# Attention inputs of all four sequences in one stage, and the last mixture, norm and store of all four sequences in one stage

## The chip, the cores and the metric

The kernel runs on one core of a Trainium2 chip. The metric is the device time of one launch in microseconds (us). Before the change it is 2777.98 us, the median of three runs (2776.31 to 2781.35).

## What is computed

The input x holds 4 sequences of 1024 positions with 128 features. It passes through four residual blocks, each of which works on the layer-normalised x: a gated linear recurrence with a feed-forward part, a mixture of 16 experts of which each position uses two, a softmax attention with rotary positions, and a last block with its own attention, a norm and a mixture of 8 experts. Cut to what matters here:

```python
x = x + _L0_attn_ref(_layernorm(x), ...)          # recurrence and feed-forward
x = x + _L0_ffn_ref(_layernorm(x), ...)           # 16 experts, two per position
x = x + _L1_attn_ref(_layernorm(x), ...)          # attention, 16 heads of 8
x = x + _L1_ffn_ref(_layernorm(x), ...)           # attention, norm, 8 experts, norm
...
q, k = _rope(proj(Wq, bq)), _rope(proj(Wk, bk))
v = proj(Wv, bv)
scores = jnp.einsum('bhtd,bhsd->bhts', q, k) / scale
out = jnp.einsum('bhts,bhsd->bhtd', jax.nn.softmax(scores, axis=-1), v)
...
x1 = _layernorm(x + attn_out, g1, be1)
return _layernorm(x1 + moe_out, g2, be2)
```

## The kernel before

The program is a row of **stages**. A stage (`stage`, L65) opens semaphores, gives each engine a block of instructions, and ends with a barrier of all engines (L78), after which GpSimd's (POOL's) `sem_clear` has freed the semaphores. Inside a stage each engine goes through its own instructions strictly in the order written, and waits only on semaphores. Engines are PE (TensorE), DVE (VectorE), ACT (ScalarE), POOL (GpSimd) and SP (the queue that issues the direct DMAs).

Both layers of attention run through L1235 to L1284. "Layer 0" below is the first of the two, "layer 1" the second. A layer has these stages before attention proper:

1. The first (L1252): SP loads `cos` and `sin`, in layer 0 DVE sets two rows that SP stores eight times, and POOL fills `v_ext` with ones (L1274).
2. In layer 0 alone, `fetch_first` (L1220): POOL gathers the experts' answers of sequence 0, 16 indirect DMAs (`fetch`, L611), and waits for them.
3. `attention_inputs(b)` (L709), once per sequence. DVE first combines the gathered answers with x in layer 0 (`combine`, L621: 8 + 8 instructions on `w_now`), then computes the norm (`norm_vector`, L96). PE transposes the 8 tiles of `xn` (`norm_tensor`), ACT copies them to `y_t` in two halves, PE projects four **jobs** (q and k, each in two halves of 512 positions; two matmuls of 512 columns per job, L736), then v (L739). DVE turns each job by the rotary angles (`ra` L756, `rb` L759, `rot` L764). ACT rounds `rot` to the high part (`qh`, `kh`, L810), POOL subtracts it for the low part (`ql`, `kl`, L784), and SP stores the parts to the DRAM tensor `qk_parts`, six DMAs of 512 KB per sequence. The buffers `ra`, `rb`, `rot` hold two jobs, so that DVE starts job n only after POOL has made the low part of job n - 2:

```python
                if n >= 2:
                    dve.wait_ge(summed, n - 1)
                    dve.wait_ge(low, n - 1)
```

POOL's order in this stage is: the 16 gathers of the next sequence (layer 0), or in the last sequence the memsets of `qs` and `ks` (L790, L791), then the residual plus bias (L794), then the four low parts, and at last a wait for the gathers.

Attention proper (L850) is one stage for all sequences, and starts with SP's loads from `qk_parts` (L881, L882). Its end and the second mixture of experts follow. The end of the program is `fetch_first` again, and then `finish(b)` (L677), one stage per sequence: DVE combines, norms, scales and adds (L705), SP stores, while POOL gathers the answers of the next sequence and waits for them.

Of the kernel before, what the change touches and what calls it, by code (L numbers as in the profile page):

```python
# [14 lines left out]
P = 128  # L15
# [13 lines left out]
PART_STORES = 6  # L29
# [139 lines left out]
def take_low_inputs(dve, t, high):  # L169

    for h in range(NH):
        dve.wait_ge(high, h + 1)
        s = slice(h * HALF, (h + 1) * HALF)
        dve.tensor_tensor(t["y_low"][:, s], t["y_f"][:, s], t["y_high"][:, s].bitcast(F32), ALU.subtract)

# [435 lines left out]
def fetch(pool, t, b):  # L611

    for i in range(NT):
        for k in range(2):
            pool.indirect_dma_start(t["back"][:, b % 2, i, k, :], None, t["answers"],  # L615
                                    bass.IndirectOffsetOnAxis(ap=t["slot_of"][:, b * NT + i, k:k + 1], axis=0))\
                .then_inc(t["fetched"], 16)
            t["fetches"] += 16

def combine(dve, t, b, copied, mixed, out, base):  # L621

    dve.tensor_copy(t["w_now"][:, :, :], t["wt"][:, bass.ds(b * NT, NT), :]).then_inc(copied, 1)  # L623
    dve.wait_ge(copied, 1)
    for i in range(NT):
        dve.scalar_tensor_tensor(t["mixed"][:, i, :], t["back"][:, b % 2, i, 0, :], t["w_now"][:, i, 0:1],  # L626
                                 base(i, 1).rearrange("p a d -> p (a d)"), ALU.mult, ALU.add).then_inc(mixed, 1)
    for i in range(NT):
        dve.wait_ge(mixed, i + 1)
        dve.scalar_tensor_tensor(out(i, 1).rearrange("p a d -> p (a d)"), t["back"][:, b % 2, i, 1, :],  # L630
                                 t["w_now"][:, i, 1:2], t["mixed"][:, i, :], ALU.mult, ALU.add).then_inc(mixed, 1)
    dve.wait_ge(mixed, 2 * NT)
# [44 lines left out]
def finish(nc, t, b):  # L677

    xn, x2, x = t["xn"], t["x2"], t["x"]  # L680
    with stage(nc, *NORM, "copied", "mixed", "added") as (block, *sems, copied, mixed, added):
        @block.sync
        def _(sp):
            for h in range(NH):
                sp.wait_ge(added, h + 1)
                sp.dma_start(t["out_v"][b, :, h * TPH:(h + 1) * TPH, :], x(h * TPH, TPH))\
                    .then_inc(t["out_stored"], 16)

        @block.gpsimd
        def _(pool):  # L690
            if b + 1 < B:
                fetch(pool, t, b + 1)
                pool.wait_ge(t["fetched"], t["fetches"])

        @block.scalar
        def _(act):
            norm_scalar_root(act, t, sems)

        @block.vector
        def _(dve):  # L700
            combine(dve, t, b, copied, mixed, lambda i, n: xn[:, i:i + n, :], t["n_view"])
            norm_vector(dve, t, sems, xn, x2, row_gain=t["row"]("g2"), row_shift=t["row"]("be2"))
            dve.wait_ge(sems[3], NT)
            for h in range(NH):
                dve.tensor_tensor(x(h * TPH, TPH), x(h * TPH, TPH), x2[:, h * TPH:(h + 1) * TPH, :],  # L705
                                  ALU.add).then_inc(added, 1)

def attention_inputs(nc, t, w, layer, a, b):  # L709
# [4 lines left out]
    jobs = [(k, h) for k in range(2) for h in range(NH)]  # L714
    with stage(nc, *NORM, "proj_done", "rot_used", "summed", "high", "low", "v_done", "rot_a", "copied", "mixed") as \
            (block, *sems, proj_done, rot_used, summed, high, low, v_done, rot_a, copied, mixed):

        stored, before = t["parts_stored"], PART_STORES * 16 * (B * layer + b)

        @block.sync  # L720
        def _(sp):
            for k, (first, second, third) in enumerate((("qh", "qh", "ql"), ("kh", "kl", "kh"))):
                for i, part in enumerate((first, second, third)):
                    sp.wait_ge(low if part in ("ql", "kl") else high, NH * (k + 1))
                    sp.dma_start(t["parts"][b, k, :, i * DH:(i + 1) * DH, :],
                                 a[part][:, :].bitcast(F32)).then_inc(stored, 16)

        @block.tensor
        def _(pe):
            norm_tensor(pe, t, sems, t["xn"], 6)  # L730
            for n, (k, h) in enumerate(jobs):
                if n >= 2:
                    pe.wait_ge(rot_used, n - 1)
                pe.wait_ge(sems[5], h + 1)
                for i, m in enumerate(((wq, wqr), (wk, wkr))[k]):
                    pe.matmul(psum[:, 2 * (n % 2) + i, :], m, t["y_t"][:, h * HALF:(h + 1) * HALF],  # L736
                              start=True, stop=True).then_inc(proj_done, 1)
            for i in range(NT):
                last = pe.matmul(psum[:, 4 + i // TPH, (i % TPH) * P:(i % TPH + 1) * P], t["y_t"][:, i * P:(i + 1) * P],  # L739
                                 wv, start=True, stop=True)  # L740
                if i % TPH == TPH - 1:
                    last.then_inc(v_done, 1)

        @block.vector
        def _(dve):
            if layer == 0:
                combine(dve, t, b, copied, mixed, t["x"], t["x"])
            norm_vector(dve, t, sems, t["x"](), t["xn"])
            for n, (k, h) in enumerate(jobs):
                s = slice(h * HALF, (h + 1) * HALF)  # L750
                name = "qk"[k]
                dve.wait_ge(proj_done, 2 * n + 1)
                if n >= 2:
                    dve.wait_ge(summed, n - 1)
                    dve.wait_ge(low, n - 1)
                dve.scalar_tensor_tensor(a["ra"][:, n % 2, :], psum[:, 2 * (n % 2), :], col(f"att{layer}_b{name}"),  # L756
                                         t["cos"][:, s], ALU.add, ALU.mult).then_inc(rot_a, 1)
                dve.wait_ge(proj_done, 2 * n + 2)
                dve.scalar_tensor_tensor(a["rb"][:, n % 2, :], psum[:, 2 * (n % 2) + 1, :],  # L759
                                         col(f"att{layer}_b{name}r"), t["sin"][:, s],  # L760
                                         ALU.add, ALU.mult).then_inc(rot_used, 1)
                dve.wait_ge(rot_a, n + 1)
                dve.wait_ge(rot_used, n + 1)
                dve.tensor_tensor(a["rot"][:, n % 2, :], a["ra"][:, n % 2, :], a["rb"][:, n % 2, :],  # L764
                                  ALU.add).then_inc(summed, 1)
            for h in range(NH):
                dve.wait_ge(v_done, h + 1)
                bias = t["rows"][:, ROWS[f"att{layer}_bv"]:ROWS[f"att{layer}_bv"] + 1, :].to_broadcast([P, TPH, D])
                dve.tensor_tensor(t["v_ext"][:, b * NT + h * TPH:b * NT + (h + 1) * TPH, 0:HEADS * VE]
                                  .rearrange("p i (h c) -> p i h c", c=VE)[:, :, :, 0:DH],  # L770
                                  psum[:, 4 + h, :].rearrange("p (i h d) -> p i h d", i=TPH, d=DH),
# [610 lines left out]
```

## Time and profile before

| what | value |
|---|---|
| median of three runs | 2777.98 us |
| the profiled execution's own time | 2800.65 us |
| its span, first to last instruction | 2799.4 us |
| PE, DVE, ACT, POOL busy share | 78%, 75%, 54%, 18% |
| DVE maxima in attention (L1048) | 1253.9 us in 2048 instructions |
| ACT exponentials in attention (L1028) | 1110.8 us in 2048 instructions |
| POOL gathers of answers (L615) | 133.2 us in 128 instructions |
| POOL memsets of `v_ext`, `qs`, `ks` (L1274, L790, L791), mean of one | 4551, 3511, 6950 ns, two of each |
| projections (L736), mean of one record | 702 ns, 128 records |

In the timeline a row such as "x8" merges equal instructions that follow each other; a wait of DVE on PEq or POOLq at L69 or L78 is the barrier between two stages.

### The profile page before, as it was taken

To read this page: it belongs to the slowest core of one execution; us is meant where nothing else is said; L and a number is where in the kernel's file an instruction comes from. 1 tells how busy PE (TensorE), PEld (TensorE's weight loads), DVE (VectorE), ACT (ScalarE), POOL (GpSimd) and SP (SyncE) were. 2 spreads that over 40 slices of the span, in tenths; PEclk is the share of its full clock that TensorE was granted. 3 is DMA by queue.
4 is the path that set the end of the run, shared out by engine and by line. 5 is a ranking of instruction groups with operands and counts; after the bars stand their busy time and mean duration, and the time that the engine had idled before them with its cause. 6 is when DMAs were issued, how large, how long until landed. Compare 5 with 4: busy or idle time off the path is not lost. (4 is left out here: it accounts for less than half of the span.)

```text
span 2799.4 us, 47294 instructions
## 1 busy us (share of the span) xinstructions
PE 2189.5 (78%) x17224; PEld 1196.2 (43%) x17224; DVE 2107.7 (75%) x4605; ACT 1502.4 (54%) x2898; POOL 504.2 (18%) x410
## 2 busy tenths in 40 slices
PE   6888965772339999999999549999999999458910
PEld 5667744661123333333333223333333333348910
DVE  6667767462568999999996568999999997375635
ACT  4433430240105888888888215888888888304510
POOL 2223310555630000000000230000000000006544
PEclk9999975896657999999999767999999999658965
DMA  4000000242330000000000330000000000202211
GB/s 173 0 0 0 0 24 14 68 82 73 117 112 13 25 14 25 25 14 25 20 7 1 106 121 17 25 13 25 22 17 25 13 14 2 97 8 62 68 45 53
DMA packets 64576, 109.71 MB, mean 39 GB/s; under 512 B 10352, under 2 KB 44272, under 8 KB 64112
## 3 DMA queue, kind: packets, MB, share of 16 engines
q1 hardware_dynamic: 55408, 88.60, 9.3%
q0 software_dynamic: 8960, 18.37, 2.7%
q8 instruction: 127, 2.08, 0.3%
q14 instruction: 81, 0.66, 0.1%
HBM read 64.46 MB, written 41.94 MB: 38 GB/s over the span
## 5 line engine op out<-in xcount | busy, mean ns | idle before, releaser
L1048 DVE TENSOR_REDUCE mh<-psum 128x1 f32<-128x512 f32 x2048 | 1253.9, 682 | 87.2 <-PE psum L923 78.1
L1028 ACT ACTIVATE p<-psum 128x512 f32<-128x512 f32 x2048 | 1110.8, 596 | 205.9 <-PE psum L957 168.1
L923 PE MATMUL psum<-ks,qs 64*128 64x512 f32 x2048 | 767.2, 462 | 35.0 <-DMA ks<-qk_parts 34.3
L957 PE MATMUL psum<-qs,ks 64*128 64x512 f32 x2048 | 749.9, 446 | 2.4 <-ACT p L1028 2.4
L969 PE MATMUL psum<-p,v_ext 128*32 128x256 f32 x8192 | 656.4, 392 | 34.4 <-ACT p L1028 34.4
L957 PEld LDWEIGHTS psum<-qs,ks 64*128 64x128 f32 x2048 | 303.8, 186 | 392.1 <-ACT p L1028 352.8
L923 PEld LDWEIGHTS psum<-ks,qs 64*128 64x128 f32 x2048 | 312.5, 190 | 65.6 <-DMA ks<-qk_parts 34.7
L969 PEld LDWEIGHTS psum<-p,v_ext 128*32 128x32 f32 x8192 | 162.1, 108 | 413.0 <-issue 234.7
L157 PE MATMUL psum<-ident,xn 128*128 128x128 f32 x160 | 44.3, 455 | 264.4 <-DVE xn L125 220.6
L575 ACT ACTIVATE hid<-psum,stage 128x128 f32<-128x128 f32 x448 | 131.9, 366 | 207.1 <-issue 111.2
L519 POOL DMA_INDIRECT x_in<-n_rows,token_of x152 | 167.1, 1099 | 274.1 <-POOLq L78 183.7
L545 PE MATMUL psum<-x_t,stage 128*128 128x128 f32 x896 | 138.6, 292 | 25.2 <-issue 15.7
L615 POOL DMA_INDIRECT back<-answers,slot_of x128 | 133.2, 1041 | 101.9 <-issue 54.0
L649 POOL COPY n_all<-xn 128x1024 f32 x4 | 4.2, 1039 | 797.6 <-DVE xn L132 797.6
L157 PEld LDWEIGHTS psum<-ident,xn 128*128 128x128 f32 x160 | 29.4, 190 | 276.1 <-DVE xn L125 224.0
L1274 POOL MEMSET v_ext<- 128x5344 f32 x2 | 9.1, 4551 | 757.5 <-POOLq L78 757.5
L598 DVE COPY stage<-ew 128x642 f32 (+1 forms) x152 | 95.3, 627 | 65.6 <-DVE y_out L590 47.3
L555 PE MATMUL psum<-stage,hid 128*128 128x128 f32 x896 | 128.8, 280 | 10.7 <-ACT hid L575 6.0
L545 PEld LDWEIGHTS psum<-x_t,stage 128*128 128x128 f32 x896 | 116.3, 198 | 40.2 <-issue 24.8
L229 PE MATMUL psum<-y_high,w_high 128*128 128x512 f32 x256 | 106.3, 415 | 20.2 <-PEq L78 20.2
L555 PEld LDWEIGHTS psum<-stage,hid 128*128 128x128 f32 x896 | 115.2, 196 | 12.1 <-ACT hid L575 6.8
L138 ACT ACTIVATE std<-var 128x8 f32<-128x8 f32 (+1 forms) x29 | 6.1, 210 | 210.9 <-DVE var L110 186.8
(172 smaller groups left out, 2405.6 us busy)
## 6 DMA issues: line engine op xcount, KB each, us to landing
qs<-qk_parts SPq DMA_DIRECT2D x128, 100.0 KB
ks<-qk_parts SPq DMA_DIRECT2D x128, 100.0 KB
answers<-y_out SPq DMA_DIRECT2D x152, 64.0 KB
qk_parts<-qh SPq DMA_DIRECT2D x16, 512.0 KB, 4.4
qk_parts<-kh SPq DMA_DIRECT2D x16, 512.0 KB, 4.3
ew<-in_moe SPq DMA_DIRECT2D x1, 5136.0 KB, 18.1
ew<-in_moe SPq DMA_DIRECT2D x1, 4624.0 KB, 13.8
n_rows<-xn SPq DMA_DIRECT2D x8, 512.0 KB, 3.2
```

The lines of the kernel that those rows point to most:

```text
L229: last = pe.matmul(psum[:, n % BANKS, :], a[:, m, c * P:(c + 1) * P], t[y][:, h * HALF:(h + 1) * HALF], start=(k == 0), stop=(k == 2))
L519: pool.indirect_dma_start(t["x_in"][:, i % NX, :], None, t["n_rows"], bass.IndirectOffsetOnAxis(ap=t["token_of"][:, i:i + 1], axis=0))\
L545: last = pe.matmul(psum[:, 2 + i % 2, f * P:(f + 1) * P], t["stage"][:, i % NST, W1 + f * P:W1 + (f + 1) * P], t["x_t"][:, i % 2, :], star ...
L555: last = pe.matmul(psum[:, 4 + i % 2, 0:P], t["hid"][:, i % 2, f, :], t["stage"][:, i % NST, W2 + f * P:W2 + (f + 1) * P], start=(f == 0), ...
L575: act.activation(t["hid"][:, i % 2, f, :], psum[:, 2 + i % 2, f * P:(f + 1) * P], func, bias=t["stage"][:, i % NST, B1 + f:B1 + f + 1]).th ...
L598: dve.tensor_copy(t["stage"][:, i % NST, :], t["ew"][:, bass.ds(e, 1), :] .rearrange("p a c -> p (a c)")).then_inc(staged, 1)
L615: pool.indirect_dma_start(t["back"][:, b % 2, i, k, :], None, t["answers"], bass.IndirectOffsetOnAxis(ap=t["slot_of"][:, b * NT + i, k:k + ...
L923: pe.matmul(psum[:, bank, :], a["qs"][r, g % NKF, i * P:(i + 1) * P], a["ks"][r, g % NKF, j % KM, k * HALF:(k + 1) * HALF], start=True, st ...
L957: pe.matmul(psum[:, S_BANK + n % NS, :], a["ks"][r, g % NKF, j % KM, i * P:(i + 1) * P], a["qs"][r, g % NKF, h * HALF:(h + 1) * HALF], sta ...
L969: last = pe.matmul(psum[GR * j:GR * j + VW, O_BANK, q], t["v_ext"][:, b * NT + i, VE * (h0 + j):VE * (h0 + j) + VW], a["p"][:, (GH * s + j ...
L1028: act.activation(a["p"][:, n % NP, :], psum[:, S_BANK + n % NS, :], ACT.Exp, scale=DH ** -0.5)\
L1048: dve.tensor_reduce(a["mh"][:, g % 2, c, k:k + 1], psum[:, bank, :], AX.X, ALU.max).then_inc(used, 1)
```

## The change

`attention_inputs` becomes one stage for all four sequences of a layer, and `finish` one stage for all four. The separate first stages (loads, memsets, `fetch_first`) are gone: their work moves into these. In detail:

- POOL's fill of `v_ext` and its memsets of `qs` and `ks` move to DVE, in layer 0 only, and stand at the start of the stage. Layer 1 keeps the contents.
- POOL's residual plus bias moves to the start of attention's stage; DVE waits for it (`summed`) only before the sequence's last addition there.
- The norm is written straight to `n_all`, ACT's copy of the transposed tiles to one of two buffers (`y_t`, `y_b`). The weights of `combine` are read from `wt`, without the copy to `w_now`.
- The high and low parts have three buffers, one per **pair** (sequence, q or k). ACT waits for the stores of pair p - 3 before it writes pair p.
- The gathers have a semaphore per buffer, on which DVE waits. POOL gathers sequence b + 2 as soon as DVE has combined sequence b.
- Each engine has an order over the sequences, written out below.

```diff
-def finish(nc, t, b):
...
+def finish(nc, t, x, n):
...
         @block.gpsimd
         def _(pool):
-            if b + 1 < B:
-                fetch(pool, t, b + 1)
-                pool.wait_ge(t["fetched"], t["fetches"])
+            for b in range(B):
+                if b >= 2:
+                    pool.wait_ge(mixed, 2 * NT * (b - 1))
+                fetch(pool, t, b)
...
+            for b in range(B):
+                wait_for_fetch(dve, t, 1, b)
+                combine(dve, t, b, mixed, lambda i, n: xn[:, i:i + n, :], n[b], 2 * NT * b)
+                norm_steps(dve, t, link, (var_ready, std_ready, normed), b, xn, x2)
...
-def attention_inputs(nc, t, w, layer, a, b):
+def attention_inputs(nc, t, w, layer, a):
...
+            def turn(b):
+                for i in range(NT):
+                    if b and i % TPH == 0:
+                        pe.wait_ge(y_copied, NH * (b - 1) + i // TPH + 1)
+                    pe.wait_ge(tile_ready, NT * b + i + 1)
...
+            def project(b):
+                y = a["y"][b % 2]
+                for n in range(JB * b, JB * (b + 1)):
+                    _, k, h = jobs[n]
+                    if n >= 2:
+                        pe.wait_ge(rot_used, n - 1)
+                    pe.wait_ge(y_copied, NH * b + h + 1)
...
+            for b in range(B):
+                turn(b)
+                project(b)
...
+            if layer == 0:
+                dve.memset(a["ra"][0:HEADS, :, :], 0.0).then_inc(row_set, 1)
+                dve.memset(a["rb"][0:HEADS, :, :], -1.0).then_inc(row_set, 1)
+                dve.memset(t["v_ext"][:, :, :], 1.0)
+                dve.memset(a["qs"][:, :, :].bitcast(F32), 0.0)
+                dve.memset(a["ks"][:, :, :, :].bitcast(F32), 0.0)
+            norm(0)
+            dve.wait_ge(loaded, 32)
+            if layer == 0:
+                dve.wait_ge(rows_stored, 16 * 2 * B)
+            for b in range(B):
+                if b + 1 < B:
+                    norm(b + 1)
+                rotate(b)
...
+            if layer == 0:
+                for b in range(2):
+                    fetch(pool, t, b)
+            for b in range(B):
+                if layer == 0 and b + 2 < B:
+                    pool.wait_ge(mixed, 2 * NT * (b + 1))
+                    fetch(pool, t, b + 2)
+                take_low(b)
...
+            def copy_turned(b):
+                act.wait_ge(var_ready, b + 1)
+                act.activation(t["std"][:, 0:1, :], t["var"][:, 0:1, :], ACT.Sqrt).then_inc(std_ready, 1)
+                if b >= 2:
+                    act.wait_ge(v_done, NH * (b - 1))
+                for h in range(NH):
+                    act.wait_ge(turned, NT * b + TPH * (h + 1))
+                    act.activation(a["y"][b % 2][:, h * HALF:(h + 1) * HALF], psum[:, T_BANK + h, :], ACT.Copy)\
+                        .then_inc(y_copied, 1)
...
+            copy_turned(0)
+            for b in range(B):
+                if b + 1 < B:
+                    copy_turned(b + 1)
+                take_high(b)
...
+        @block.gpsimd
+        def _(pool):
+            for b in range(B):
+                v = a["sum"][b]()
+                pool.tensor_tensor(v, v, t["row"](f"att{layer}_bo"), ALU.add).then_inc(summed, 1)
```

ACT before, the stages of sequences 0 and 1 of layer 0 (L138 is the root of the norm, L148 the copy of the transposed tiles, L810 the high parts):

```order
L138 ACT_TABLE_LOAD
L138 ACTIVATE std<-var 128x8
L148 ACTIVATE y_t<-psum 128x512 x2
L810 ACTIVATE qh<-rot 128x512 x2
L810 ACTIVATE kh<-rot 128x512 x2
L69 UNCONDITIONAL_BRANCH
L801 UNCONDITIONAL_BRANCH
L138 ACTIVATE std<-var 128x8
L148 ACTIVATE y_t<-psum 128x512 x2
L810 ACTIVATE qh<-rot 128x512 x2
L810 ACTIVATE kh<-rot 128x512 x2
```

ACT now, all four sequences of layer 0 (L891 the root, L896 the copy, L906 the high parts):

```order
L891 ACT_TABLE_LOAD
L891 ACTIVATE std<-var 128x8
L896 ACTIVATE y_t<-psum 128x512 x2
L891 ACTIVATE std<-var 128x8
L896 ACTIVATE y_b<-psum 128x512 x2
L906 ACTIVATE hi<-rot 128x512 x4
L891 ACTIVATE std<-var 128x8
L896 ACTIVATE y_t<-psum 128x512 x2
L906 ACTIVATE hi<-rot 128x512 x4
L891 ACTIVATE std<-var 128x8
L896 ACTIVATE y_b<-psum 128x512 x2
L906 ACTIVATE hi<-rot 128x512 x8
```

The root and the copies of sequence b + 1 stand ahead of the high parts of sequence b now; those of sequences 2 and 3 follow each other.

POOL before, layer 0 from the fill to the end of sequence 0's stage:

```order
L1274 MEMSET v_ext 128x5344
L69 UNCONDITIONAL_BRANCH
L76 ISA
L1224 UNCONDITIONAL_BRANCH
L615 DMA back<-answers,slot_of 128x128 x16
L69 UNCONDITIONAL_BRANCH
L774 UNCONDITIONAL_BRANCH
L615 DMA back<-answers,slot_of 128x128 x16
L794 TENSOR_TENSOR x_all<-x_all,rows 128x1024
L784 TENSOR_TENSOR ql<-rot,qh 128x512 x2
L784 TENSOR_TENSOR kl<-rot,kh 128x512 x2
```

POOL now, all of layer 0's stage and the start of attention's:

```order
L638 DMA back<-answers,slot_of 128x128 x48
L875 TENSOR_TENSOR lo<-rot,hi 128x512 x4
L638 DMA back<-answers,slot_of 128x128 x16
L875 TENSOR_TENSOR lo<-rot,hi 128x512 x12
L69 UNCONDITIONAL_BRANCH
L76 ISA
L974 UNCONDITIONAL_BRANCH
L978 TENSOR_TENSOR x_all<-x_all,rows 128x1024 x4
```

The gathers of three sequences stand ahead of the first low part, and those of the fourth ahead of sequence 1's low parts.

## Rows read from the trace of the kernel before

**Rows 1.** Timeline, layer 0, first stage: start us, us, engine, line, operation, [idle <-releaser]
```profile
634.51 4.55 POOL L1274 MEMSET v_ext<- 128x5344 f32 x1 [15.12 <-POOLq L78]
...
635.85 0.91 DVE L1270 MEMSET rb<- 16x1024 f32 x1 [0.16 <-issue]
```

**Rows 2.** Timeline, layer 0, stage of sequence 0, POOL and DVE
```profile
669.78 1.04 POOL L615 DMA_INDIRECT back<-answers,slot_of  x1 [3.17 <-POOLq L78]
...
671.49 2.19 DVE L630 SCALAR_TENSOR_TENSOR x_all<-back,w_now,mixed 128x128 f32<-128x128 f32 x8
...
672.43 2.06 POOL L615 DMA_INDIRECT back<-answers,slot_of  x1 [0.30 <-issue]
...
693.03 2.36 POOL L794 TENSOR_TENSOR x_all<-x_all,rows 128x1024 f32<-128x1024 f32 x1
...
695.33 2.49 POOL L784 TENSOR_TENSOR ql<-rot,qh 128x512 fp32r<-128x512 f32 x2
...
696.73 0.75 DVE L756 SCALAR_TENSOR_TENSOR ra<-psum,cols,cos 128x512 f32<-128x512 f32 x1 [9.32 <-POOL ql L784]
...
702.23 1.26 POOL L784 TENSOR_TENSOR kl<-rot,kh 128x512 fp32r<-128x512 f32 x1 [1.29 <-ACT kh L810]
```

**Rows 3.** Timeline, layer 0, stage of sequence 3, the rotation and attention's first load
```profile
798.19 0.75 DVE L756 SCALAR_TENSOR_TENSOR ra<-psum,cols,cos 128x512 f32<-128x512 f32 x1 [2.30 <-PE psum L736]
...
799.84 0.75 DVE L759 SCALAR_TENSOR_TENSOR rb<-psum,cols,sin 128x512 f32<-128x512 f32 x1 [0.90 <-PE psum L736]
...
801.97 0.74 DVE L759 SCALAR_TENSOR_TENSOR rb<-psum,cols,sin 128x512 f32<-128x512 f32 x1
...
803.87 0.74 DVE L756 SCALAR_TENSOR_TENSOR ra<-psum,cols,cos 128x512 f32<-128x512 f32 x1
...
804.78 1.95 PE L739 MATMUL psum<-att,y_t 128*128 128x128 f32 x16
...
808.98 1.27 DVE L769 TENSOR_TENSOR v_ext<-psum,rows 128x512 f32<-128x512 f32 x2
...
813.52 0.87 SPq L881 DMA_DIRECT2D qs<-qk_parts  x1
```

**Rows 4.** Timeline, layer 1, from the first stage to attention's first load
```profile
1553.48 4.55 POOL L1274 MEMSET v_ext<- 128x5344 f32 x1 [742.42 <-POOLq L78]
...
1558.82 1.65 DVE L105 BATCH_NORM_STATS2 stats<-x_all 128x6 f32<-128x128 f32 x8 [6.14 <-PEq L78]
...
1562.67 2.14 DVE L125 TENSOR_SCALAR xn<-x_all,mv,rstd 128x128 f32<-128x128 f32 x8
...
1581.97 1.65 DVE L105 BATCH_NORM_STATS2 stats<-x_all 128x6 f32<-128x128 f32 x8 [3.24 <-PEq L78]
...
1633.70 5.97 DVE L119 TENSOR_SCALAR tmp<-tmp 128x8 f32<-128x8 f32 x1
...
1659.70 0.39 SPq L881 DMA_DIRECT2D qs<-qk_parts  x1
```

**Rows 5.** Groups by line (busy, mean ns); windows (busy by engine, PEclk, DMA share, GB/s)
```profile
L229 PE MATMUL psum<-y_high,w_high 128*128 128x512 f32 x256 | 106.3, 415 | 20.2 <-PEq L78 20.2
...
L148 ACT ACTIVATE y_t<-psum 128x512 f32<-128x512 f32 x32 | 19.1, 597 | 73.4 <-PE psum L157 72.5 <-issue 0.9
...
1588.00:1589.00 1.00, 1.00 (x3) 0.64 (x3) 0.00 (x0) 0.57 (x2) 0.96 (x1) 0.50 0.00 0
...
1591.00:1592.00 1.00, 1.00 (x3) 0.40 (x2) 0.20 (x2) 0.00 (x0) 0.00 (x0) 0.75 0.00 0
```

**Rows 6.** Timeline, the last stages, gathers and the last combination
```profile
2676.59 0.94 POOL L615 DMA_INDIRECT back<-answers,slot_of  x1 [22.89 <-PEq L69]
...
2695.94 0.94 POOL L615 DMA_INDIRECT back<-answers,slot_of  x1 [2.16 <-issue]
...
2701.22 1.04 POOL L615 DMA_INDIRECT back<-answers,slot_of  x1 [3.09 <-PEq L69]
...
2782.45 2.19 DVE L626 SCALAR_TENSOR_TENSOR mixed<-back,w_now,n_all 128x128 f32<-128x128 f32 x8
```

More of the change, by code:

```diff
@@ L699, in _ @@
         @block.vector
         def _(dve):
[L701 to L706, printed above, removed]
-def attention_inputs(nc, t, w, layer, a, b):
+            link = chain(dve, step)
@@ L712, in attention_inputs, with wait_for_pair @@
+def wait_for_pair(eng, t, layer, pair):
+    uses = len(range(pair % PAIRS, 2 * B, PAIRS))
+    eng.wait_ge(t["pair_stored"][pair % PAIRS], 48 * (layer * uses + pair // PAIRS + 1))
+def attention_inputs(nc, t, w, layer, a):
     psum, col = t["psum"], t["col"]
     wq, wk, wqr, wkr, wv, wo = w.att[layer]
[L714 to L718, printed above, removed]
+    jobs = [(b, k, h) for b in range(B) for k in range(2) for h in range(NH)]
+    JB = 2 * NH
+    T_BANK, V_BANK = 6, 4
+    with stage(nc, "loaded", "row_set", "rows_stored", "mixed", "step", "var_ready", "std_ready", "tile_ready", "turned",
+               "y_copied", "proj_done", "rot_a", "rot_used", "summed", "high", "low", "v_done", "v_used") as \
+            (block, loaded, row_set, rows_stored, mixed, step, var_ready, std_ready, tile_ready, turned,
+             y_copied, proj_done, rot_a, rot_used, summed, high, low, v_done, v_used):
@@ L720, in _ @@
         @block.sync
         def _(sp):
[L722 to L726, printed above, removed]
+            sp.dma_start(t["cos"][:, :], a["cos_in"]).then_inc(loaded, 16)
@@ L766, in _ @@
[L766 to L771, printed above, removed]
-                                  bias.rearrange("p i (h d) -> p i h d", d=DH), ALU.add)
+            link = chain(dve, step)
@@ L787, in _ @@
-            if layer == 0 and b + 1 < B:
-                fetch(pool, t, b + 1)
-            if b == B - 1:
-                pool.memset(a["qs"][:, :, :].bitcast(F32), 0.0)
-                pool.memset(a["ks"][:, :, :, :].bitcast(F32), 0.0)
-            pool.wait_ge(sems[3], NT)
-            pool.tensor_tensor(t["sum"](), (t["x"]() if layer == 0 else t["xn"][:, :, :]),
-                               t["row"](f"att{layer}_bo"), ALU.add)
-            for n in range(len(jobs)):
-                take_low(n)
@@ L798, in _, with take_low @@
-            if layer == 0 and b + 1 < B:
-                pool.wait_ge(t["fetched"], t["fetches"])
+            def take_low(b):
+                for n in range(JB * b, JB * (b + 1)):
+                    _, k, h = jobs[n]
+                    s = slice(h * HALF, (h + 1) * HALF)
+                    pair = 2 * b + k
+                    pool.wait_ge(high, n + 1)
+                    pool.tensor_tensor(a["lo"][:, pair % PAIRS, s], a["rot"][:, n % 2, :],
+                                       a["hi"][:, pair % PAIRS, s].bitcast(F32), ALU.subtract).then_inc(low, 1)
@@ new lines, in take_high @@
+            def take_high(b):
+                for n in range(JB * b, JB * (b + 1)):
+                    _, k, h = jobs[n]
+                    pair = 2 * b + k
+                    act.wait_ge(summed, n + 1)
+                    if pair >= PAIRS:
+                        wait_for_pair(act, t, layer, pair - PAIRS)
+                    act.activation(a["hi"][:, pair % PAIRS, h * HALF:(h + 1) * HALF], a["rot"][:, n % 2, :], ACT.Copy)\
+                        .then_inc(high, 1)
+            copy_turned(0)
@@ L815 @@
+            for b in range(B):
+                if b + 1 < B:
+                    copy_turned(b + 1)
+                take_high(b)
 UN = GH * NT
@@ L1019, in copy_o @@
                         .then_inc(o_copied, 1)
-            act.wait_ge(t["parts_stored"], PART_STORES * 16 * B * (layer + 1))
+            for pair in range(2 * B - PAIRS, 2 * B):
+                wait_for_pair(act, t, layer, pair)
             for s in range(nsteps):
```

267 lines of the change are left out of this document (138 added, 129 removed).

## Prediction

> **What bounds the kernel now.** I read the page first: the maxima and exponentials of attention proper fill most of the span, and the change leaves them alone. What it touches are three stretches: layer 0 from the fill of `v_ext` to attention's first load, 634.51 to 813.52 [rows 1, 3], which is 179.0 us; layer 1, 1553.48 to 1659.70 [rows 4], 106.2 us; and the end, from the first gather at 2676.59 [rows 6] to the end of the span. The timeline of each shows who is last. Whatever such a stretch loses comes off the end, because attention and the experts start behind a barrier.
>
> In layer 0, POOL is last: sequence 0's stage starts its gathers at 669.78 and leaves them at 693.03, and DVE waits 9.32 us for the first low part [rows 2]. In layer 1 there are no gathers. DVE is the longest chain: a norm from 1558.82 to 1564.81, 6.0 us, then the wait for PE and the rotation, then 3.24 us of barrier [rows 4]. In the last stages POOL's gathers set the pace again [rows 6].
>
> **Pieces.** (a) Sixteen gathers alone: 14 and a pause last 2676.59 to 2695.94, two more make 21.85 us. In sequence 0's stage, beside DVE, they take 23.25 us [rows 2]; one gather beside DVE's combination takes 2.06 instead of 0.94 us. In the last stages: 2701.22 to 2782.45 are three stages of 27.2 us, each with a gap of 3.1 us before its gathers [rows 6], so 24.1, with the 0.3 between gathers 24.3 us. (b) Combination and norm: eight instructions of L630 take 2.19 us [rows 2], L626 is alike, so 4.3, and with the norm 10.3 us. (c) The four low parts once the gathers are over: 695.33 to 703.49, 8.2 us [rows 2]; DVE's third job starts 1.4 us into it and DVE ends, 6.0 us on, 0.8 us before POOL. (d) A rotation with nothing late: 798.19 to 810.25, less the 0.90 us for PE, 11.2 us; the third job starts 4.8 us after the first [rows 3]. From there to attention's first load 3.3 us. (e) From the last gather to its landing: the gap of 3.1 us holds landing and barrier together; that bounds landing between 0 and 3.1, and I take 1.4.
>
> **The new wait.** ACT now has the copies of sequence b + 1's transposed tiles ahead of sequence b's high parts. Those copies need PE's `turn(b + 1)`, which stands behind all of `project(b)`, whose third and fourth jobs need the banks that DVE frees in `rotate(b)`. So in sequences 0 to 2 DVE's third job waits for low(b, first), behind ACT, behind PE. Let T be the start of the rotation. DVE frees the first bank pair at T + 1.5 and the second at T + 3.6. A record of 512 columns at full clock takes 0.415 us [rows 5], and a job has four. PE is idle during the norm ahead of the rotation. Before, after such a norm (1581.97 to 1588.0, PE begins with its first tile at 1586.2, [rows 4]) the granted clock was 0.50, or 1.2 GHz, in 1588 to 1589 and rose only within 1591 to 1592 [rows 5]. So I take half clock for the first 5.3 us: third job T + 1.6 to 4.9, fourth to 7.7, v 1.95 us [rows 3] to 9.7, then the transposes (0.6 us for the first four) and two copies of 0.6 us [rows 5] to 11.6, the high part about 0.65, the low part 1.3 [rows 2]: DVE's third job starts at T + 13.7, not 4.8. What follows is 5.9 us, the 6.4 of [rows 3] less 0.5, as the second low part is early. A rotation is thus 19.6 us for b = 0, 1, 2, and 11.2 for b = 3. At full clock it would be some 17.5: that is the low end, and 11.2 the bound below it, if ACT were never late.
>
> **Layer 0.** The first gather starts at 634.5 [rows 1], beside the memsets. Those are now on DVE: the two of 1024 elements and 17632 elements more. The second small one takes 0.91 us, and started 1.07 us after the first [rows 1], which makes 15.7 to 18.4 us for the large ones, done by 655.5 at most. The gathers of sequence 0 end at 656.1 and land at 657.5, so the memsets cost nothing, with some 2 us of cover. If DVE locked POOL out meanwhile, they would cost up to 18.4. No row has a gather beside a DVE memset. But the small ones ran beside POOL's fill, which took 4.55 us for 5344 elements [rows 1], 0.85 ns each, as the fill of `ks` did with no DVE memset near (6950 ns for 8192, in the table): I take 0 and keep 18.4. Then: norm(0) to 667.7. Gathers of sequence 1 from 656.3 to 679.6, landed 680.7, norm(1) to 691.0. Gathers of sequence 2 to 702.8; ACT's chain gives high(0) at 691.0 + 12.2 = 703.2, just about as late; low parts to 711.5, DVE 710.7. Gathers of 3 to 734.7 cover norm(2) and the ACT chain (721.0 + 12.2); low parts to 742.9, DVE 742.1. Norm(3) to 752.4, rotate(2), uncovered, to 772.0, rotate(3) to 783.2, first load 786.5. **Gain 813.5 - 786.5 = 27.0 us.** The addition L794 (2.36 us per stage, [rows 2]) is no longer on POOL's path; in attention its four run while DVE needs POOL for nothing until the first sequence's end.
>
> The SBUF — State Buffer page of the Trainium skill (Who interferes with whom) lets a DVE instruction with at most one SBUF input outside its 2-port modes run beside GpSimd; by that the memsets cost nothing too, and no row here shows gathers beside them. For DVE instructions with two SBUF inputs the same section says that they hold up GpSimd's reads but (inferred) not descriptor writing. The trace has a gather of 2.06 us beside L630, so I keep the measured 23.25; by the rule as inferred each later batch would be 21.85 and layer 0 another 4 us shorter.
>
> **Layer 1.** DVE from 1553.5: four norms 24.0, three rotations 58.8, one 11.2, start and tail 3.5: 1651.0 against 1659.70. **Gain 8.7 us.** In it are gains of 5.3 (first stage), 3 x 3.2 (barriers), about 4 x 2.3 (DVE's wait for PE before a rotation), and the POOL memsets, beside which DVE's L119 took 5.97 us instead of 0.17 [rows 4] (with one more, 6.8), and against them three times 8.4 for ACT's order. The stores are 3 MB per 25.6 us, fewer per us than the 23.2 of a stage before [rows 4], so three pair buffers suffice, except perhaps at the end, where two rotations follow each other: ACT's wait for pair p - 3 could cost some us there, up to 5.
>
> **The end.** 21.85 + 3 x 24.3 after 2676.6 is 2771.3; the last gather ends 0.3 earlier and lands at 2772.4, where DVE's last combination starts, not at 2782.45 [rows 6]. What follows is the same 17 us. **Gain 10.0 us.** `w_now` and barriers go with it. Each buffer is free in time: combination b is over 6 us after its gathers land, the refill comes 24 us after.
>
> **Sum.** 27.0 + 8.7 + 10.0 = 45.7 us. Against the profiled execution, 2800.65 - 45.7 = 2755.0. The median of the runs stands 22.7 us below that execution, with the same instructions, so I take the same difference: 2777.98 - 45.7 = **2732 us**.
>
> **Rivals.**
> - *ACT's order costs little* (PE keeps full clock, or the transposes come early): with rotations of 17.5 us the four uncovered ones give back 8.4 us, 2724; with 11.2, 33.6 us, 2699. For it: PE is cheap. Against it: the order on PE and ACT leaves no way round, only the clock is open. 2724 lies in my range; the chance that it ends below 2715 is 0.10.
> - *DVE's memsets lock POOL out.* Then sequence 0's gathers end 18.4 us later and all of layer 0 with them: 2751. Chance 0.10.
> - *Slower: unpaced gathers pay a pause each.* The pause of 2.16 us after 14 gathers [rows 6] could be a full descriptor queue that drains. Now gathers follow each other without a drain: 48, 16 and 64 in a row. If each beyond the fourteenth of a run pays 2.16 - 0.30 = 1.86, these are 34 + 2 + 50 = 86, 160 us; eight pauses are in my sum already, 15 us. 2732 + 145 = 2877, slower. It decides from 0.6 us per gather up (45.7/78). Against it: gathers 15 and 16 of a batch follow at 0.3 us again, right after the pause. Chance 0.04.
>
> **Numbers.** Forecast 0.75, the rivals as given, 0.01 for no change. Faster by over 0.2% (5.6 us, about what a measurement of this kernel can tell from no change): 0.95; the same: 0.01; slower: 0.04. The range reaches from 2715 (full clock, lighter contention at the gathers, landing at once) to 2751 (the lock).
>
> **What would show it.** Layer 0's first load near 786, its gathers' batches of 22 to 24 us back to back with one pause each, DVE idle about 9 us before the third job of rotations 0 to 2 in layer 1, with PE at half clock before it, and none in rotation 3; L119 at 0.17 us; the last combination at 10 us less from the first gather. Gathers above 2 us through the first 20 us would show the lock, a pause before every gather the full queue. DVE's third job on time would prove my main deduction wrong.

## The result

The change takes **2727.36 us** (2725.25 to 2728.84, four runs) against 2777.14 us of the kernel before in the same comparison: a ratio of 0.982, 95% interval 0.980 to 0.984, or 49.8 us less. Forecast were 2732 us, 45.7 us less, and a range of 2715 to 2751.

The profiled execution of the change took 2726.42 us, with a span of 2724.6 us. That is 74.8 us less than the span of before, and 25 us more than the medians differ by. The difference is not the change's. By the first and last rows of each stretch:

| stretch | before | change | difference | forecast |
|---|---|---|---|---|
| up to layer 0's first gather or fill | 634.5 | 616.9 | -17.6 | 0 |
| layer 0, to attention's first load | 179.0 | 152.6 | **-26.4** | -27.0 |
| attention of layer 0 | 740.0 | 738.9 | -1.1 | 0 |
| layer 1, to attention's first load | 106.2 | 91.5 | **-14.7** | -8.7 |
| attention, second experts, to the first gather at the end | 1016.9 | 1009.6 | -7.3 | 0 |
| the end | 122.8 | 115.1 | **-7.7** | -10.0 |

The three stretches that the change touches give 48.8 us, as the medians do within their spread. The other 26.0 us lie in front of and behind them, mostly in the experts' tiles. They belong to the machine on which the profile was taken and not to the kernel. The version `finish_only` below is the kernel before in everything ahead of its end, and its profile, taken on a machine where the kernel before has a median of 2775.89 us, reaches the fill of layer 0 at 614.4 us instead of 634.5 and takes 1011.2 us instead of 1016.9 between layer 1 and the end. Another version ran on two machines, with medians of 2688.5 and 2710.5 us, and its profiles differ by 16.9 us up to layer 0 and by 6.8 us between layer 1 and the end, by 1.8 us the other way in layer 0, and nowhere else by over 0.6 us. Carrying the sum over to the median as a difference was right.

In layer 0 the gain has two parts. Up to the start of the last gather the change is 33.8 us shorter (133.7 us before, 99.9 us now); from there to attention's first load it is 7.4 us longer (45.3 us before, 52.7 us now), and in that part lies rotation 2, whose third job is late.

The page of the change, busy time by engine and two of its groups:

```profile
PE 2199.8 (81%) x17224; PEld 1193.6 (44%) x17224; DVE 2106.6 (77%) x4600; ACT 1501.6 (55%) x2898; POOL 473.7 (17%) x404
...
L1159 DVE TENSOR_REDUCE mh<-psum 128x1 f32<-128x512 f32 x2048 | 1253.9, 683 | 86.7 <-PE psum L1033 77.6
...
L638 POOL DMA_INDIRECT back<-answers,slot_of x128 | 133.7, 1044 | 90.7 <-issue 53.7
```

The work is the same as before, the maxima to 0.1 us; POOL has lost its fills (30 us for two layers). What went from the engines' rows is idle time.

The timeline of the change in layer 0 (the columns are those of [rows 1]). The first rows answer to [rows 1, 2], those from 736.63 on show why DVE's third job is late, the last ones answer to [rows 3]:

```profile
616.88 0.94 POOL L638 DMA_INDIRECT back<-answers,slot_of  x1 [13.96 <-POOLq L78]
630.00 6.88 DVE L857 MEMSET ks<- 128x8192 f32 x1 [1.66 <-issue]
...
636.29 0.94 POOL L638 DMA_INDIRECT back<-answers,slot_of  x1 [2.24 <-issue]
640.14 2.19 DVE L651 SCALAR_TENSOR_TENSOR x<-back,wt,x_all 128x128 f32<-128x128 f32 x8 [3.26 <-DMA back<-answers,slot_of]
...
663.95 2.19 DVE L651 SCALAR_TENSOR_TENSOR x<-back,wt,x_all 128x128 f32<-128x128 f32 x8 [13.46 <-DMA back<-answers,slot_of]
674.19 0.74 DVE L834 SCALAR_TENSOR_TENSOR ra<-psum,cols,cos 128x512 f32<-128x512 f32 x1
686.20 2.48 POOL L875 TENSOR_TENSOR lo<-rot,hi 128x512 fp32r<-128x512 f32 x2 [1.14 <-ACT hi L906]
687.59 0.75 DVE L834 SCALAR_TENSOR_TENSOR ra<-psum,cols,cos 128x512 f32<-128x512 f32 x1 [9.08 <-POOL lo L875]
693.47 2.93 DVE L651 SCALAR_TENSOR_TENSOR x<-back,wt,x_all 128x128 f32<-128x128 f32 x8
719.18 0.75 DVE L834 SCALAR_TENSOR_TENSOR ra<-psum,cols,cos 128x512 f32<-128x512 f32 x1 [10.42 <-POOL lo L875]
725.06 2.87 DVE L651 SCALAR_TENSOR_TENSOR x<-back,wt,x_all 128x128 f32<-128x128 f32 x8
735.97 0.75 DVE L834 SCALAR_TENSOR_TENSOR ra<-psum,cols,cos 128x512 f32<-128x512 f32 x1
...
737.43 6.43 PE L800 MATMUL psum<-y_t,att 128*128 128x512 f32 x8 [10.49 <-DVE rb L837]
743.70 1.95 PE L806 MATMUL psum<-att,y_t 128*128 128x128 f32 x16
745.49 1.04 PE L789 MATMUL psum<-ident,n_all 128*128 128x128 f32 x8
746.18 1.08 ACT L896 ACTIVATE y_b<-psum 128x512 f32<-128x512 f32 x2 [13.35 <-PE psum L789]
747.15 1.15 ACT L906 ACTIVATE hi<-rot 128x512 fp32r<-128x512 f32 x2
747.86 2.49 POOL L875 TENSOR_TENSOR lo<-rot,hi 128x512 fp32r<-128x512 f32 x2 [21.91 <-ACT hi L906]
749.25 0.75 DVE L834 SCALAR_TENSOR_TENSOR ra<-psum,cols,cos 128x512 f32<-128x512 f32 x1 [8.96 <-POOL lo L875]
```

DVE's fills end at 636.88, and DVE still waits 3.26 us for the gathers. From 736 on, the chain reads downwards: PE projects the third and fourth jobs of sequence 2 for 6.4 us, then makes v, then the transposes of sequence 3; then ACT copies these, and only then ACT makes the high part that was ready to be made at 738.2. DVE's third job starts 13.3 us after the first. In rotation 0 it starts 13.4 us after the first, but there GpSimd was still at its gathers until 685.05, and the row at 686.20 shows that it then waited only 1.14 us for ACT. In rotation 1 GpSimd went from its last gather to the low part without a wait.

Layer 1 answers to [rows 4]. The small instruction that took 5.97 us in one norm of before takes 0.17 us here:

```profile
1508.38 1.64 DVE L182 BATCH_NORM_STATS2 stats<-x_all 128x6 f32<-128x128 f32 x8 [0.72 <-PEq L78]
1511.83 0.17 DVE L193 TENSOR_SCALAR tmp<-tmp 128x8 f32<-128x8 f32 x1
...
1599.90 0.34 SPq L991 DMA_DIRECT2D qs<-qk_parts  x1
```

The windows (columns of [rows 5]) show PE's clock, first in rotation 2 of layer 0, then in rotations 0 and 1 of layer 1:

```profile
736.00:742.00 6.00, 4.57 (x6) 1.97 (x7) 4.08 (x7) 0.00 (x0) 0.00 (x0) 0.50 0.00 0
...
1524.00:1528.00 4.00, 4.00 (x26) 3.04 (x26) 0.53 (x1) 0.00 (x0) 0.00 (x0) 1.00 0.00 0
...
1544.00:1548.00 4.00, 3.67 (x5) 1.59 (x6) 2.98 (x5) 0.00 (x0) 0.00 (x0) 0.50 0.02 4
1548.00:1552.00 4.00, 4.00 (x24) 2.88 (x23) 0.00 (x0) 0.00 (x0) 0.00 (x0) 0.94 0.00 0
```

At the end (answering to [rows 6]), a batch's longest gather and DVE's instructions beside it, and the last combination:

```profile
2609.53 0.94 POOL L638 DMA_INDIRECT back<-answers,slot_of  x1 [22.92 <-PEq L69]
...
2634.78 2.18 DVE L655 SCALAR_TENSOR_TENSOR xn<-back,wt,mixed 128x128 f32<-128x128 f32 x8
2635.19 2.59 POOL L638 DMA_INDIRECT back<-answers,slot_of  x1 [0.30 <-issue]
...
2707.05 2.19 DVE L651 SCALAR_TENSOR_TENSOR mixed<-back,wt,n_all 128x128 f32<-128x128 f32 x8 [10.61 <-DMA back<-answers,slot_of]
```

### The profile page after: what moved, and what is told of

Read it like the earlier page. It is cut to its first block and busy times, and to the rows that moved or that the text cites. A ratio compares the mean times of both kernels' runs of the same rounds, so it can differ in the third digit from the quotient of the medians.

```text
span 2724.6 us, 46987 instructions
## 1 busy us (share of the span) xinstructions
PE 2199.8 (81%) x17224; PEld 1193.6 (44%) x17224; DVE 2106.6 (77%) x4600; ACT 1501.6 (55%) x2898; POOL 473.7 (17%) x404
## 5 line engine op out<-in xcount | busy, mean ns | idle before, releaser
L875 POOL TENSOR_TENSOR lo<-rot,hi 128x512 fp32r<-128x512 f32 x32 | 40.2, 1266 | 837.0 <-ACT hi L906 837.0
L638 POOL DMA_INDIRECT back<-answers,slot_of x128 | 133.7, 1044 | 90.7 <-issue 53.7
L252 PE MATMUL psum<-y_high,w_high 128*128 128x512 f32 x256 | 106.5, 416 | 19.6 <-PEq L78 19.6
L326 POOL TENSOR_TENSOR gated<-state,qg 128x512 f32<-128x512 f32 x64 | 82.3, 1286 | 146.8 <-DVE qg L306 137.2
L252 PE MATMUL psum<-y_low,w_high 128*128 128x512 f32 x256 | 102.0, 398 | 0.0
L252 PE MATMUL psum<-y_high,w_low 128*128 128x512 f32 x256 | 101.6, 397 | 0.0
## 6 DMA issues: line engine op xcount, KB each, us to landing
ew<-in_moe SPq DMA_DIRECT2D x1, 5136.0 KB, 18.3
```

What stands on the lines that cost most here:

```text
L252: last = pe.matmul(psum[:, n % BANKS, :], a[:, m, c * P:(c + 1) * P], t[y][:, h * HALF:(h + 1) * HALF], start=(k == 0), stop=(k == 2))
```

## The experiments

All times are medians; a comparison's kernel before is given where it matters. Edits are to the change unless another kernel is named. In this section layer 0 is counted from the stage's first load, 0.6 us ahead of the first gather, so that the change's own is 153.3 us.

**The end alone** (`finish_only`): the kernel before, with the change's `finish` and its gathers.

> The kernel before, with only the end changed as in the change: combination, norm and store of all four sequences in one stage; layers 0 and 1 as before. My theory, the end's own gain adds to the rest: 7.7 us less in the traces (115.1 instead of 122.8 us from the first gather to the end), 8 to 10 by the sum, so 2768 us against 2777 of the kernel before; the trace shows four batches of gathers with one pause each and the first of them some 97 us ahead of the last combination. Rival, the end gains only because the stages before it have drained the queue or changed its state: no change here, 2777.

Measured: 2768.38 us against 2775.89, ratio 0.997 (0.996 to 0.998). In the trace the end takes 114.9 us, and layers 0 and 1 take 181.2 and 106.3 us, near the 179.0 and 106.2 of before. The end's gain is its own, 7.5 to 7.9 us, and adds up with the rest.

**ScalarE's order** (`act_order`):

```diff
-                if b + 1 < B:
-                    copy_turned(b + 1)
+                if b + 1 < B:
+                    root(b + 1)
                 take_high(b)
+                if b + 1 < B:
+                    copy_turned(b + 1)
```

> The change with ScalarE's order turned: the root of sequence b + 1, then all four high parts of b, and only then the copies of b + 1's transposed tiles. My theory (the third job of rotations 0 to 2 waits for ScalarE, which waits for TensorE's transposes behind the projection): layer 1 loses 16.9 + 18.6 + 18.3 - 3 x 11.2 = 20.2 us, layer 0 9.5 us (8.1 in rotation 2, 1 in rotation 0, where the gathers bound), but rotation 3 now waits for its projections behind those copies, 2 to 3 us in each layer: 2727 - 25 = 2702. Rival, TensorE at half clock is what the third job waits for and the order is innocent: the jobs' bank pairs come no earlier, at most 5 us, 2722 or more.

**TensorE's order** (`pe_order`): the transposes of sequence 0 stand ahead of the loop, and those of b + 1 inside `project(b)`, behind its second job:

```diff
+                    if n == JB * b + 1 and b + 1 < B:
+                        turn(b + 1)
```

> The change with TensorE's order turned instead: the transposes of b + 1 stand behind the first two jobs of b's projection, ahead of the third and fourth and of v; ScalarE's order is that of the change. My theory: the copies are done about 2 us after the norm, ahead of the first high part, so the third job starts 4.8 to 5.5 us after the first in all rotations, and rotation 3 has its projections in time: 2727 - 29 = 2698, a few us below the version with ScalarE's order turned. Rival, the transposes at half clock (2.3 us) now hold up the third job: rotations of 13 to 14 us, 2710.

Measured: 2705.30 us for ScalarE's order and 2700.32 us for TensorE's, ratios 0.975 (0.974 to 0.976) and 0.973 (0.972 to 0.974), each 2 to 3 us above what I expected. Both rivals are out: it is the order that the third job waits for, and TensorE's clock only adds to it. Layer 1 shrinks from 91.5 us to 73.4 and 71.0 (18.1 and 20.5 us). DVE of the second version in layer 1, first and third job, no wait:

```profile
1531.09 0.74 DVE L836 SCALAR_TENSOR_TENSOR ra<-psum,cols,cos 128x512 f32<-128x512 f32 x1
...
1535.76 0.74 DVE L836 SCALAR_TENSOR_TENSOR ra<-psum,cols,cos 128x512 f32<-128x512 f32 x1
```

Of ScalarE's order, rotation 3 starts with a wait for its projection, as deduced:

```profile
1562.37 0.75 DVE L834 SCALAR_TENSOR_TENSOR ra<-psum,cols,cos 128x512 f32<-128x512 f32 x1 [1.23 <-PE psum L800]
```

Layer 0 gives less than I expected: 4.5 and 5.6 us, where rotation 2 alone gives 8.6. The pause inside the third batch of gathers grew from 2.29 us to 4.20 us in the first version and 3.85 us in the second:

```profile
685.05 0.94 POOL L638 DMA_INDIRECT back<-answers,slot_of  x1 [3.85 <-issue]
687.27 2.49 POOL L877 TENSOR_TENSOR lo<-rot,hi 128x512 fp32r<-128x512 f32 x2
688.67 0.75 DVE L836 SCALAR_TENSOR_TENSOR ra<-psum,cols,cos 128x512 f32<-128x512 f32 x1 [10.79 <-POOL lo L877]
```

So rotation 1 was GpSimd's all along and rotation 0 but for 1.1 us, and their third jobs became about 2 us later rather than 1 us earlier. No run tries why the pause grew. The traces give a hint: in layer 0 of all versions, each of the nine pauses of 2.9 to 4.9 us had two stores of high parts issued in the 4 us before it began, and the other pauses (2.15 to 2.36 us) had none, or one issued less than 0.6 us ahead of it.

**The fills on GpSimd** (`mem_pool`): the three large fills moved ahead of its first gather.

> The change with the fills of v_ext, qs and ks on GpSimd, ahead of layer 0's gathers, instead of on VectorE. My theory: GpSimd's gathers are the path up to the last batch, and VectorE's fills were hidden under them, so the 15 to 16 us of fills (0.85 ns per element, 17632 elements) come on top nearly whole: 2727 + 15 = 2742. Rival, VectorE's fills slow the gathers down or stand in the way of the first combination and so cost part of what they take: less than 10 us more.

Measured: 2741.66 us, ratio 0.988 (0.986 to 0.989), 14.3 us more than the change. Layer 0 takes 167.4 us instead of 153.3, nearly the 15.0 us that the fills take GpSimd. So GpSimd is the path there, and VectorE's fills, which this version does without, cost about 1 us at most in the change.

**The fills twice on VectorE** (`mem_twice`):

```diff
+                link(dve.memset(t["v_ext"][:, :, :], 1.0))
+                link(dve.memset(a["qs"][:, :, :].bitcast(F32), 0.0))
+                link(dve.memset(a["ks"][:, :, :, :].bitcast(F32), 0.0))
                 dve.memset(t["v_ext"][:, :, :], 1.0)
```

> The change with the three large fills of VectorE in layer 0 done twice. My theory, VectorE waits for the gathers there and its fills are hidden: 18 us more of fills start the first combination at 655 instead of 640 us, and the second, which waited 13.5 us for its gathers, 1 to 2 us later than now; the rest moves by that: 2729. Rival, VectorE's fills hold GpSimd's gathers back or VectorE is the path: 2742 to 2745.

Measured: 2736.16 us, ratio 0.986 (0.984 to 0.988), 8.8 us more than the change: neither my theory nor the rival. VectorE's delay was absorbed, but one gather wasn't left alone:

```profile
648.68 9.03 POOL L638 DMA_INDIRECT back<-answers,slot_of  x1 [0.30 <-issue]
649.86 6.88 DVE L860 MEMSET ks<- 128x8192 f32 x1 [1.66 <-issue]
656.66 2.06 DVE L651 SCALAR_TENSOR_TENSOR x<-back,wt,x_all 128x128 f32<-128x128 f32 x8
...
672.83 2.19 DVE L651 SCALAR_TENSOR_TENSOR x<-back,wt,x_all 128x128 f32<-128x128 f32 x8 [5.97 <-DMA back<-answers,slot_of]
```

The gather ends 0.97 us after the fill, and the second combination still waits 5.97 us for gathers: the 8.1 us of that gather are the cost in the trace, close to the 8.8 us of the medians.

**The fills twice, in another order** (`mem_order`): the first time as before, the second time `ks`, `qs`, `v_ext`:

```diff
+                link(dve.memset(t["v_ext"][:, :, :], 1.0))
+                link(dve.memset(a["qs"][:, :, :].bitcast(F32), 0.0))
+                link(dve.memset(a["ks"][:, :, :, :].bitcast(F32), 0.0))
+                dve.memset(a["ks"][:, :, :, :].bitcast(F32), 0.0)
+                dve.memset(a["qs"][:, :, :].bitcast(F32), 0.0)
                 dve.memset(t["v_ext"][:, :, :], 1.0)
```

> The three large fills twice, as before, but the first time in the order ks, qs, v_ext. The same work for VectorE, so the same end of the fills, near 655. What held one gather 9.03 us beside the second fill of ks is open; theory A, that fill holds a gather whenever one is under way as it starts: with two of them, at 619 to 626 and at 650 to 657, one gather each, of 7 to 9 us, and the second as before: 2735 to 2743. Theory B, it takes more than that (in the change and in the version before, three gathers ran at 0.94 us beside the first fill of ks), and it is a chance of the order: the time lies anywhere from 2729 to 2737, and at most one gather is long.

The expectation says that the first round is in the new order; the edit turned the second one. The two fills of `ks` therefore follow each other, and don't stand at the times that the expectation gives. Both start with a gather under way, so the run still decides between the theories.

Measured: 2760.36 us against 2812.10, ratio 0.982 (0.980 to 0.983), as the change's own; the interval is too wide for the 4.2 us that layer 0 takes more in the trace (157.5 us). Theory A is out: no gather is held by either fill of `ks`, and one by the last fill of `v_ext`, again until 0.96 us after its end:

```profile
657.65 0.94 POOL L638 DMA_INDIRECT back<-answers,slot_of  x1 [0.30 <-issue]
657.83 6.88 DVE L858 MEMSET ks<- 128x8192 f32 x1 [1.77 <-issue]
...
670.05 4.51 DVE L860 MEMSET v_ext<- 128x5344 f32 x1 [1.06 <-issue]
670.14 5.38 POOL L638 DMA_INDIRECT back<-answers,slot_of  x1 [0.30 <-issue]
```

That is theory B as far as it goes: what picks the gather stays open.

**GpSimd's fills in layer 1** (`fills_1`): `qs` and `ks` filled again by GpSimd at that stage's start.

> The change with the fills of qs and ks done once more, by GpSimd, at the start of layer 1's stage, where GpSimd has nothing to do: 10.5 us of GpSimd beside VectorE's norms. My theory (the small instructions of the norm stand still beside GpSimd's fills, as L110 with 1.14 us and L119 with 5.97 us did in the kernel before): 6.8 us more, 2734. Rival, those two records were long for another reason, and an idle engine's fill costs nothing: 2727.

Measured: 2735.20 us, ratio 0.986 (0.984 to 0.988), 7.8 us more; layer 1 takes 98.7 us instead of 91.5. The two durations of before come back to the last digit:

```profile
1508.74 3.51 POOL L879 MEMSET qs<- 128x4096 f32 x1 [729.46 <-POOLq L78]
...
1511.13 1.14 DVE L187 TENSOR_SCALAR var<-mv 128x8 f32<-128x8 f32 x1
1512.19 6.95 POOL L880 MEMSET ks<- 128x8192 f32 x1
...
1512.99 0.17 DVE L192 TENSOR_TENSOR tmp<-tmp,var 128x8 f32<-128x8 f32 x1
1513.19 5.97 DVE L193 TENSOR_SCALAR tmp<-tmp 128x8 f32<-128x8 f32 x1
```

Each TENSOR_SCALAR of 8 elements ends within 0.03 us of the end of GpSimd's fill; TENSOR_TENSOR and RECIPROCAL beside it don't stop. So the removal of the fills of layer 1 is worth the 6.8 us that the prediction gave them (these two rows), or 7.2 us by the stretch.

> The change with twice the room for descriptors (4096 instead of 2048). Theory, the pause of 2.2 us once per 16 gathers is a full ring that drains, and twice the room halves their number: of eight pauses of 1.9 us extra in the gathers of layer 0 and of the end, four go, 7 to 8 us, and a few in the experts: 2719. Rival, the pause is of the instruction stream and has nothing to do with the room: 2727 and the same pauses. I hold both for equally likely.

Measured: 2712.37 us, ratio 0.978 (0.976 to 0.979), 15.0 us less than the change. All eight pauses of layer 0 and the end are gone, not half; layer 0 gains 6.9 us, the end 7.7. In layer 0, gathers 15 and 16, the first of which had the pause before it:

```profile
635.07 0.94 POOL L638 DMA_INDIRECT back<-answers,slot_of  x1 [0.30 <-issue]
636.31 0.94 POOL L638 DMA_INDIRECT back<-answers,slot_of  x1 [0.30 <-issue]
```

**Low parts on VectorE** (`dve_low`): on top of TensorE's order, VectorE makes the low parts of sequences 0 and 1 in layer 0, job n's behind `rot` of job n + 1.

> The version with TensorE's order turned, and in layer 0 the low parts of sequences 0 and 1 computed by VectorE (behind the next job's rotation) instead of GpSimd. My theory, GpSimd's 4 x 23 us of gathers and 2 x 8.2 us of low parts are the path up to the last combination: the gathers now follow each other, the last combination starts some 13 us earlier, VectorE has room for 4.5 us more per rotation, 2700 - 11 = 2689. Rival, VectorE becomes the bound, or its instructions with two inputs in SBUF slow the gathers by as much: 2697 or more.

Measured: **2688.47 us** against 2774.52, ratio 0.969 (0.967 to 0.971). Layer 0 takes 135.2 us instead of 147.7. As expected, to 1 us. This version beats both kernels, by 86 and by 39 us.

**Both** (`dve_low_ring`), in a comparison in which the kernel before took 2812.10 us:

> The version with TensorE's order turned and VectorE's low parts in layer 0, and with room for descriptors of 4096. My theory (pauses gone, each worth 1.9 us where gathers are the path): at the end all four count, 7.6 us; in layer 0 three count, as the fourth combination there waits for VectorE and not for its gathers, 5.7 us: 2688.5 - 13.3 = 2675. Rival, without pauses the gathers meet more of VectorE's instructions and give part of it back: 2680 or more.

Measured: 2741.64 us, ratio 0.974 (0.972 to 0.975), worse than without. Layer 0 takes 160.8 us. The end takes 114.8 us, as without the room, although its code is that of `ring` (107.4 us) and no gather has a pause; VectorE stands still twice there:

```profile
2705.05 1.69 DVE L182 BATCH_NORM_STATS2 stats<-xn 128x6 f32<-128x128 f32 x8 [7.38 <-remote]
2713.48 0.84 DVE L185 BATCH_NORM_AGGREGATE mv<-stats 128x2 f32<-128x6 f32 x8 [6.74 <-remote]
```

So both versions were run again, together, on a third machine:

> The version with TensorE's order turned and VectorE's low parts in layer 0 once more, as the control of the next one on the same chip: 0.969 of the kernel before, 2688 where that takes 2775. In the comparison of the version with more room, the kernel before took 2812 us, and VectorE stood for 9 us three times in layer 0; this one without the room for descriptors tells whether the chip or the room did that. If the chip: here too some 30 us more in layer 0 on a chip like that one, and nothing on the other kind. If the room: none here on either.

> The same with room for descriptors of 4096, again. Theory A (on a chip where the kernel before takes 2775, gathers leave VectorE its instructions, and the pauses saved are the whole difference): 13 us less than the control, 2675. Theory B (without pauses the gathers starve VectorE wherever it runs this version): 20 us more than the control, 2708 or above, with standstills of 9 us in VectorE's row in layer 0.

Measured: 2710.50 and 2729.34 us against 2800.67; ratios 0.968 (0.967 to 0.970) and 0.975 (0.973 to 0.976). Theory B: on one machine, the room does it. Layer 0 takes 133.4 us without and 159.9 with it, the end 115.0 and 106.5. DVE in the version with more room, while GpSimd issues a gather every 1.25 us:

```profile
686.30 1.67 DVE L182 BATCH_NORM_STATS2 stats<-x_all 128x6 f32<-128x128 f32 x8 [4.16 <-remote]
...
697.01 0.95 POOL L638 DMA_INDIRECT back<-answers,slot_of  x1 [0.30 <-issue]
697.49 0.58 DVE L185 BATCH_NORM_AGGREGATE mv<-stats 128x2 f32<-128x6 f32 x7 [9.53 <-remote]
...
707.99 0.17 DVE L187 TENSOR_SCALAR var<-mv 128x8 f32<-128x8 f32 x1 [8.93 <-remote]
```

The profile finds nothing on the core that releases DVE there. I suppose that its instructions arrive late behind the gathers' packets; no run shows it. The change's own order with the same room (`ring`) had no such row; it ran on a machine on which the kernel before takes 2774.52 us, so whether the machine or the order spared it is open. That the standstills of the first run also came at the end, in the code of `ring`, speaks against the order as the only cause.

## Why the prediction was right

- **What bounds layer 0: right.** 152.6 us from the first gather to the first load, 152.0 forecast (786.5 less 634.5), and no point on the way is off by more than 1.3 us: norm(0) ends 33.6 us after the first gather (33.2 forecast), combination 1 starts at 47.1 (46.2), rotation 0 ends at 76.7 (76.2), combination 3 starts at 108.2 (107.6). The batches of gathers beside VectorE's work took 23.7 and 22.9 us from pause to pause in layer 0, near the 23.25 us that the prediction kept. `mem_pool` shows that GpSimd's time is the path, `dve_low` that taking work from it gives it back.
- **Memsets on DVE cost nothing: right in the change, for a reason that is only partly right.** The time was hidden with 3.26 us of cover, 2 forecast. The rival's mechanism exists all the same: `mem_twice` and `mem_order` each have one gather held to the end of a fill. By the page "SBUF — State Buffer" of the Trainium skill (Who interferes with whom), a VectorE instruction with at most one SBUF input, outside the 2-port modes, doesn't contend with GpSimd, and a memset has no input; these two rows speak against it, the other 57 gathers beside fills in the traces of the change and of these two versions, all of 0.94 or 0.95 us, for it. The same section counts `tensor_scalar` among the instructions that can enter a 2-port mode, and says that in such a mode whoever comes first blocks the other for the whole instruction: `fills_1` agrees, 5.97 us instead of 0.17, though no trace shows the mode.
- **The new wait: right,** and the largest loss in the change that a run shows. DVE's third job starts 13.3 us after the first in rotation 2 of layer 0, 13.7 forecast. (The 13.4 us of rotation 0 are GpSimd's gathers but for 1.1 us, as the prediction had it: "just about as late".) The two versions with the order turned gave back 22 and 27 us, so the rival that the order costs little is wrong too.
- **Layer 1: the mechanism was right and one term too large,** the rotation of 19.6 us, which was summed at half clock everywhere. "Half clock for the first 5.3 us" held in layer 0, where PE began at 737.43 and the granted clock is 0.50 from 736 to 742.5 and 1.00 from 743 on. In layer 1 the third job came at 10.9, 12.6 and 12.4 us: the clock was 1.00 from 1524 to 1528 in rotation 0, and in rotation 1 it was 0.50 from 1544 to 1548 and 0.94 on average from 1548 to 1552. Rotations of 16.9, 18.6 and 18.3 us instead of 19.6 make 5.0 of the 6.0 us that layer 1 gained beyond the forecast; the norms make 0.5, rotation 3, barrier and tail the rest. The total came out closer than its terms by luck: layer 1 gave 6.0 us more than forecast, layer 0 0.6 us and the end 2.3 us less, 3.1 us together.
- **The end: 2.3 us too much.** The period is 24.8 us, not 24.3. The gather beside L655 takes 2.59 us where it took 2.06 beside L630 [rows 2]; three of them are 1.6 us. Landing took 1.6 us, not 1.4, and what follows the start of the last combination took 0.6 us more than before. The stage of 27.2 us from which the period was made is the distance of the gathers' starts; the two times that the prediction names for it are 81.2 us apart, 27.1 each.
- **No waits for stores: right.** In the list of waits, what ends ACT's idle time before a high part is `rot` (20 times), and never a store.
- **The slower rival: wrong.** Unpaced gathers pay one pause of 2.2 us per 16, as one batch did before. `ring` shows that the pause goes with more room for descriptors, which fits the full queue that the rival supposed, but no more than one pause per 16 gathers came, 64 in a row at the end included.

## What to carry to other kernels

When stages are merged, write down each engine's order over the iterations and look for a step of b + 1 that stands ahead of a step of b that another engine waits for; here one such inversion, ScalarE's high parts behind copies that need TensorE's transposes, cost 22 us by turning ScalarE's order and 27 by turning TensorE's, about half of what the merge gained. Judge a moved fill by what it runs beside, too: hidden time is free only while neither engine holds the other. A gain found by removing a pause should be measured in the final order and on more than one machine, as the pause may have been what let another engine go on.

## What was not expected

- The pause of 2.2 us once per 16 gathers vanishes altogether with twice the room (2.24 to 0.30 us), worth 15.0 us, and the same setting costs 18.8 us in another order of the same work on another machine (2710.5 to 2729.3).
- A gather beside two runs of VectorE's combination ends 0.8 us after the second, 2.59 us instead of 0.94; one beside a fill ends 0.96 us after it, once in each of two versions with the fills done twice, and never beside the fills of the change itself.
- The same program differs by 22 us between machines (2688.5 and 2710.5), nearly all of it in the experts' gathers and tiles.
